# The side work of the second mixers: other slots for softplus, the norm and the sums of the two directions

## What is computed

```
xz = xn @ Win;  xi, z = split(xz)                      # 512 features each
xi = silu(causal_conv4(xi) + convb)
dt_in, B, C = split(xi @ Wx)                           # 16, 16, 16
dt = softplus(dt_in @ Wdt + bdt)
h[t] = exp(dt[t] * A) * h[t-1] + dt[t] * xi[t] * B[t]  # 16 states for each feature
y[t] = sum over states of h[t] * C[t]  +  xi[t] * D
out = (y * silu(z)) @ Wout
yf = layernorm(mixer_fw(xn) + xn);  yb = layernorm(flip(mixer_bw(flip(xn))) + xn)
y = yf + yb                                            # then the feed-forward part
```

## Time and profile before

| | before |
|---|---|
| median of 3 runs | 3462.02 us |
| the profiled execution | 3458.87 us |
| its span, first to last instruction | 3457.1 us |
| mean granted TensorE clock | 0.920 of full speed |
| busy, share of the span: PE, DVE, POOL, ACT | 81%, 82%, 65%, 51% |
| the passes 0 to 7 of `mixer1` | 1000.8 to 2984.2 us |
| the mixers' tail, to the next stage's first instruction | 2984.2 to 3027.5 us |

### The profile page before, as it was taken

One profiled execution on the slowest core, in us unless ns is written; L12 is line 12 of the kernel. 1 busy time (PEld: TensorE's weight loads), 2 busy tenths in 40 slices (PEclk: granted clock), 3 DMA queues, 4 the chain that ended last, 5 costly groups with the idle time before them and its releaser, 6 DMA issues. The chain is left out here.

```text
span 3457.1 us, 25114 instructions
## 1 busy us (share of the span) xinstructions
PE 2799.2 (81%) x7782; PEld 1191.0 (34%) x7782; DVE 2831.2 (82%) x2257; ACT 1773.3 (51%) x2375; POOL 2241.1 (65%) x1102
## 2 busy tenths in 40 slices
PE   6678777666578988988888888788898897778899
PEld 2223222454223333333333333333333332234344
DVE  6999999542369999999999999999999999678300
ACT  5775776231355655655655555555555654333211
POOL 3696499001339898898888888888888989401000
PEclk8899899887789999999999999999999999989899
DMA  1011011147425454554554545544545546321000
GB/s 65 31 49 37 26 49 49 60 165 274 161 87 176 177 175 162 176 184 157 186 188 160 188 169 180 171 173 168 181 167 170 190 153 207 122 89 49 12 19 24
DMA packets 164437, 451.46 MB, mean 131 GB/s; under 512 B 22832, under 2 KB 51696, under 8 KB 164272
## 3 DMA queue, kind: packets, MB, share of 16 engines
q1 hardware_dynamic: 158544, 428.89, 36.3%
q0 software_dynamic: 5760, 20.97, 1.5%
HBM read 414.94 MB, written 34.87 MB: 130 GB/s over the span
## 5 line engine op out<-in xcount | busy, mean ns | idle before, releaser
L1398 POOL TENSOR_TENSOR mix_prod<-mix_spread,mix_h 128x1024 f32<-128x1024 f32 x512 | 1344.1, 2628 | 242.9 <-DVE mix_h L1824 161.1
L1932 PE MATMUL mix_banks<-mix_prod,kept_ident 128*128 128x512 f32 x2048 | 1041.0, 634 | 67.0 <-POOL mix_prod L1398 37.3
L1448 ACT ACTIVATE mix_side_in<-mix_dt,mix_neg_a 128x1024 f32<-128x1024 f32 x384 | 437.5, 1141 | 307.9 <-DVE mix_h L1824 304.0
L1932 PEld LDWEIGHTS mix_banks<-mix_prod,kept_ident 128*128 128x128 f32 x2048 | 401.1, 200 | 499.0 <-issue 303.6
L1810 DVE TENSOR_TENSOR mix_banks<-mix_banks,mix_dtu 128x1024 f32<-128x1024 f32 x384 | 467.2, 1217 | 8.0 <-POOL mix_dtu L1388 4.1
L1824 DVE TENSOR_TENSOR_SCAN mix_h<-mix_side_in,mix_state,mix_banks 128x1024 f32<-128x1024 f32 x192 | 450.6, 2347 | 17.8 <-issue 0.5
L1824 DVE TENSOR_TENSOR_SCAN mix_h<-mix_side_in,mix_banks 128x1024 f32<-128x1024 f32 x192 | 439.1, 2287 | 18.8 <-ACT mix_side_in L1448 1.3
L410 POOL TENSOR_TENSOR mix_drive<-mix_drive,mix_du 128x1024 f32<-128x1024 f32 x128 | 305.0, 2400 | 147.9 <-ACT mix_drive L481 147.9
L1922 PE MATMUL mix_banks<-mix_parts,kept_sel 96*128 96x512 bf16 x384 | 156.1, 407 | 233.3 <-DVE mix_h L1824 226.4
L1408 POOL TENSOR_TENSOR mix_side_in<-mix_spread,mix_dtu 128x512 f32<-128x512 f32 x256 | 339.1, 1324 | 0.2
L633 DVE TENSOR_TENSOR_SCAN mix_h<-mix_banks,mix_state,mix_drive 128x1024 f32<-128x1024 f32 x128 | 296.2, 2340 | 11.5 <-POOL mix_drive L410 5.9
(11 more groups left out here) (270 smaller groups left out, 4463.1 us busy)
## 6 DMA issues: line engine op xcount, KB each, us to landing
mix_spread<-par_rows SPq DMA_DIRECT2D x640, 512.0 KB, 4.0
mix_c_row<-c_rows SPq DMA_DIRECT2D x40, 512.0 KB, 3.6
exa_f<-f SPq DMA_DIRECT2D x32, 512.0 KB, 6.7
slot_outputs<-exa_inter POOLq DMA_DIRECT2D x32, 512.0 KB, 7.4
ln_zp<-slot_outputs SPq DMA_DIRECT2D x8, 2048.0 KB, 8.0
first_acc<-xT SPq DMA_DIRECT2D x8, 512.0 KB, 7.3
x_scratch<-first_acc POOLq DMA_DIRECT2D x8, 512.0 KB, 3.2
fw_scratch<-mix_res SPq DMA_DIRECT2D x8, 512.0 KB, 6.3
```

Of the source, the lines that this page charges most:

```text
L1398: pool.tensor_tensor(prod[:, un % 2, :], spread[:, i % SLOTS, :], h[:, un % HR, :], ALU.mult).then_inc(prod_ready, 1)
L1448: act.activation(drive[un % 2] if pooled(un) else side_in[:, un % 2, :], dt[:, at // NS, :], ACT.Exp, scale=neg_a[:, way(p), at:at + 1]).t ...
L1932: mm = pe.matmul(y_bank[:, hf, :], k.ident[:], half(prod[:, un % 2, :], hf), start=False, stop=True, skip_group_check=True)
```

## The change

Only the tables of slots change. No instruction is added, removed or altered, and every engine's buffers stay what they are.

- VectorE: softplus of group 2 goes from slots 19, 19, 20 to 19, 20, 21, of group 3 from 24, 25, 26 to 25, 26, 27. The norm of the first half: `near_root` 17 to 18, `root_of` 20 to 22, `normed` 21 and 22 to 23 and 24, `joined` 32 and 33 to 38 and 45. Of the second half: `near_root` 29 to 30, `root_of` stays at 40, `normed` 46 and 47 to 43 and 44, `joined` 48 and 49 to 51 and 52. The taps of the convolution (31 to 33, 35 to 37, 39, 41, 42) and the gates stay.
- ScalarE, TensorE and `Steps`: what feeds these goes one slot later: the dt rows of group 3 (20 to 21), the fourth `out` (22 to 23) and its copy (25 to 26), the second `var` (26 to 27) and `roots` (27 to 28), the first two `xi` (25, 27 to 26, 28), their copies and the first `first_tap`.
- GpSimd: the second half of `times_u` of group 3 goes from slot 46 to 42.
- SyncE: the first load of yf goes from slot 26 to 30, the first store from 36 to 46, the second load from 37 to 46, the second store from 53 to 54.

```diff
--- before.py
+++ after.py
@@ -1134,16 +1134,16 @@
         for p in range(-1, passes + 1):
             order = []
             if 0 <= p < passes:
-                for g, s in ((1, 1), (2, 10), (3, 20)):
+                for g, s in ((1, 1), (2, 10), (3, 21)):
                     order += [(s, h, ("dt", p, g, h)) for h in range(2)]
                 for g, at in enumerate(((12, 13), (29, 30), (44, 45), (55, 56))):
                     order += [(at[h], 2, ("z", p, g, h)) for h in range(2)]
             if p >= 1:
-                for n, s in enumerate((3, 6, 16, 22)):
+                for n, s in enumerate((3, 6, 16, 23)):
                     order.append((s, 0, ("out", p - 1, n % 2, n // 2)))
-                order += [(15, 0, ("var", p - 1, 0)), (26, 0, ("var", p - 1, 1))]
+                order += [(15, 0, ("var", p - 1, 0)), (27, 0, ("var", p - 1, 1))]
             if p + 1 < passes:
-                for n, s in enumerate((25, 27, 32, 33, 34, 36, 37, 39)):
+                for n, s in enumerate((26, 28, 32, 33, 34, 36, 37, 39)):
                     order.append((s, 0, ("xi", p + 1, n // 2, n % 2)))
                 order += [(41, 0, ("cv", p + 1, 0)), (42, 0, ("cv", p + 1, 1))]
                 order.append((47, 0, ("par", p + 1)))
@@ -1318,13 +1318,12 @@
 
             def side(p, s):
                 if p >= 1:
-                    if s == 26:
+                    if s == 30:
                         load_yf(p - 1, 0)
-                    if s == 36:
+                    if s == 46:
                         store(p - 1, 0)
-                    if s == 37:
                         load_yf(p - 1, 1)
-                    if s == 53:
+                    if s == 54:
                         store(p - 1, 1)
                 if p + 1 < NP and s == 55:
                     sp.wait_ge(c_kept, p + 2)
@@ -1411,7 +1410,7 @@
                     ins.then_inc(pooled_ready, 1)
 
             def side(p, s):
-                for g, at in ((1, (10, 14)), (2, (22, 26)), (3, (34, 46))):
+                for g, at in ((1, (10, 14)), (2, (22, 26)), (3, (34, 42))):
                     if 0 <= p < NP and s in at:
                         times_u(p, g, at.index(s))
                 if p + 1 < NP and s in (60, 62):
@@ -1596,7 +1595,7 @@
                 if own and s % NS == 2:
                     skip(p, s // NS)
                 if own:
-                    for g, s0 in ((1, 2), (2, 11), (3, 21)):
+                    for g, s0 in ((1, 2), (2, 11), (3, 22)):
                         if s == s0:
                             soft_in(p, g)
                         if s == s0 + 1:
@@ -1604,22 +1603,22 @@
                         if s == s0 + 2:
                             soft_log(p, g)
                 if behind:
-                    for n, s0 in enumerate((6, 9, 19, 25)):
+                    for n, s0 in enumerate((6, 9, 19, 26)):
                         if s == s0:
                             keep_out(p - 1, n % 2, n // 2)
                     if s == 16:
                         roots(p - 1, 0)
-                    if s == 27:
+                    if s == 28:
                         roots(p - 1, 1)
                 if ahead:
                     if p + 1 == WAY and s == 5:
                         tap_matrices(1)
-                    for n, s0 in enumerate((26, 28, 33, 34, 35, 37, 38, 40)):
+                    for n, s0 in enumerate((27, 29, 33, 34, 35, 37, 38, 40)):
                         if s == s0:
                             keep_xi(p + 1, n // 2, n % 2)
                     if s in (43, 44):
                         keep_cv(p + 1, s - 43)
-                    for g, s0 in enumerate((28, 34, 37)):
+                    for g, s0 in enumerate((29, 34, 37)):
                         if s == s0:
                             first_tap(p + 1, g)
                 for s0, gate, shaped in ((14, 0, ()), (31, 1, ()), (40, None, (0, 1)), (46, 2, (2, 3)), (57, 3, ())):
@@ -1760,7 +1759,7 @@
                 if behind:
                     if s == 2:
                         gate_y(p - 1, 3)
-                    for hf, at in enumerate(((17, 20, 21, 22, 32, 33), (29, 40, 46, 47, 48, 49))):
+                    for hf, at in enumerate(((18, 22, 23, 24, 38, 45), (30, 40, 43, 44, 51, 52))):
                         if s == at[0]:
                             near_root(p - 1, hf)
                         if s == at[1]:
@@ -1771,7 +1770,7 @@
                             if s == at[4 + c]:
                                 joined(p - 1, hf, c)
                 if own:
-                    for g, at in ((1, (7, 8, 9)), (2, (19, 19, 20)), (3, (24, 25, 26))):
+                    for g, at in ((1, (7, 8, 9)), (2, (19, 20, 21)), (3, (25, 26, 27))):
                         for part, s0 in enumerate(at):
                             if s == s0:
                                 soft(p, g, part)
@@ -1936,22 +1935,22 @@
             def side(p, s):
                 own, ahead, behind = 0 <= p < NP, p + 1 < NP, p >= 1
                 if own:
-                    for g, s0 in ((1, 1), (2, 10), (3, 20)):
+                    for g, s0 in ((1, 1), (2, 10), (3, 21)):
                         if s == s0:
                             step_rows(p, g)
                     for g, at in enumerate(((12, 13), (29, 30), (44, 45), (55, 56))):
                         if s in at:
                             zg(p, g, at.index(s))
                 if behind:
-                    for n, s0 in enumerate((3, 6, 16, 22)):
+                    for n, s0 in enumerate((3, 6, 16, 23)):
                         if s0 <= s < s0 + 3:
                             project(p - 1, n % 2, n // 2, s - s0)
                     if s == 15:
                         var(p - 1, 0)
-                    if s == 26:
+                    if s == 27:
                         var(p - 1, 1)
                 if ahead:
-                    for n, s0 in enumerate((25, 27, 32, 33, 34, 36, 37, 39)):
+                    for n, s0 in enumerate((26, 28, 32, 33, 34, 36, 37, 39)):
                         if s == s0:
                             xi(p + 1, n // 2, n % 2)
                     if s in (41, 42):
```

## The result

| | before | changed |
|---|---|---|
| median, us | 3462.1 (4 runs, 3459.9 to 3465.8) | **3426.0** (4 runs, 3421.1 to 3429.2) |
| ratio of the times | | **0.989** (95%: 0.988 to 0.991) |
| profiled execution, its time | 3458.9 | 3423.6 |
| its span | 3457.1 | 3421.8 |
| first drive of pass 0 to the last scan's start | 1981.1 | 1942.5 |

The kernel is 36 us faster; 39 were forecast as the sum, 3423 as the median. The span shows where: the passes lost 38.6 us, pass 0 began 1.7 later, the tail grew by 2.1, the last stage lost 0.6, together 35.4 (by the unrounded spans 35.3).

The account below looks back on a forecast made before the run. VectorE was taken to bound the kernel, some instructions stretched by sharing a slot with GpSimd's product. Gains of 13.9, 15.2, 7.8 and 10.0 less losses of 3.5, 2.5 and 2.1 gave 38.8 us: 3423 us, range 3412 to 3439.

Parts of the forecast that it names:

- L1707: Softplus's second part, moved from slot 19 to 20, falls to 1.20 us each in passes 1 to 7: gain 13.9 us.
- L1710: Softplus's third part, moved from slot 20 behind L1729 (`root_of`) to slot 21, falls to 1.20 us: gain 15.2 us.
- The norm: Second half's norm, moved from slots 46 and 47 to 43 and 44, loses its stretching by GpSimd's backlog: gain 7.8 us.
- Joins and taps: Joins leave slots 32 and 33, SyncE's load goes to slot 30, so convolution taps are no longer stretched: gain 10.0 us.
- The gate: With `near_root` moved behind the gate in slot 18, VectorE waits there for TensorE's sum: loss 3.5 us.
- Rival 3: TensorE isn't binding at the gate: 3.9 us gained there, 3.5 not lost; 3416 us, chance 0.10.
- The port in slots 19 to 27: Nine SBUF instructions in a row leave VectorE and GpSimd level, and VectorE pays where early: loss 2.5 us.
- rival 1: GpSimd falls behind and the port paces slots 19 to 27, 15.8 us lost in place of 2.5; 3436.5 us, chance 0.15.
- rival 2: TensorE's slow clock makes VectorE wait for spread rows once a pass in slots 12-18 or 28-31: 3434 us, chance 0.10.
- SyncE: Store of slot 46 waits for slot 45's join in passes 5 to 7; product 46 starts 1-2 us late: cost 0.
- Rival 5: GpSimd is behind throughout slots 19 to 27 and each of nine instructions pays 1.0 us: 3484 us, chance 0.04.
- The tail: After the passes, the second half's root and norm stand ahead of the first half's second join: loss 2.1 us.

Follow-up runs that it names:

- pair19: Changed kernel with softplus's second part for group 2 back in slot 19 behind the first part: 3437.6 us.
- root21: Changed kernel with `root_of` of the first half back in slot 21, together with softplus's third part: 3447.7 us.
- norm46: Changed kernel with the norm of the second half back in slots 46 and 47 and the half of `times_u` in slot 46: 3421.2 us.
- norm47: Changed kernel with the norm of the second half in slots 47 and 48, behind ScalarE's silu block: 3420.5 us.
- join32: Changed kernel with the joins of the first half back in slots 32 and 33, their store and load in 36 and 37: 3429.6 us.
- load26: Changed kernel with SyncE's first load of yf back in slot 26: 3444.1 us.
- near17: Changed kernel with `near_root` of the first half back in slot 17, ahead of the gate: 3420.9 us.
- near29: Changed kernel with `near_root` of the second half back in slot 29: 3428.0 us.
- best2: Changed kernel with `near_root` of the first half in 17, its second join in 43, the second half's norm in 47 and 48: 3415.0 us.

## Why the prediction was right

The time came out as forecast: 3426 against 3423, inside the range, in the direction given 0.94. Its terms, in its own order:

- **L1707: right.** 12.5 us for 13.9. The 1.4 missing are pass 0, where it took 1.59 and 2.31 us. `pair19` shows the cause.
- **L1710: right**, 15.2 us to the decimal; `root21` gives 15.2 back.
- **The norm: the step that failed.** The instruction was rightly sized (7.5 us for 7.8), but slots 43 to 53 took 0.2 us more where 5.7 less were forecast. The step costed the product and its port and didn't ask what is late next when VectorE comes 2.7 us sooner: the decay behind ScalarE's silu block, for which the scan of slot 48 waits 7.0 us in passes 1 to 6. This could be read beforehand. The block's two table loads stood in the trace of before, and in pass 3 the decay behind it had 1.66 us to spare where 2.7 were taken away. `norm46` and `norm47` show both sides. Pass 7 prepares no next pass and has no such wait; there L1735 met products of GpSimd in flight, took 1.05 and 1.80 us in slots 43 and 44, and the stretch grew by 1.7 us.
- **Joins and taps: right**, 10.5 us for 10.0. That a join ahead of a tap is the cause holds (`join32`, slot 33), but only where the product is on time (slot 32). In slot 45 the join took 0.83 and 1.35 us in passes 5 and 6, and without it 43 to 53 of passes 5 to 7 are 3.4 us shorter (`join32`), where 2.1 were counted. The blame put on SyncE for the taps in slot 31 is borne out by `load26`, where they take 1.71 and 1.76 us again; what the same wait costs once softplus ends a slot later was underrated by far, at 2 to 8 us for 22.
- **The gate: right.** TensorE is binding: the waits are 6.5 us over seven passes, slots 16 to 19 grew by 2.7 where 3.5 were forecast, and `near17` takes 3.1 off. Rival 3 falls.
- **The port in slots 19 to 27: oversized.** 2.5 us forecast. In passes 1 to 7 the instructions of slots 19 to 21, 26 and 27 are all at 1.20 us. The loss there is 1.7 us, in slot 25, and from another cause, TensorE's slow clock in slot 23 of three passes. So rival 1 didn't happen. Nor did rival 2 as it was put, since the waits for the spread rows fell; its cause, the slow clock, shows in another place, at 1.7 and not 10.6 us, and by way of GpSimd.
- **The bank of z: right at 0** (`near29`). **SyncE: right at 0 in the changed kernel.** Its store waited 4.4 to 5.1 us for the join in slot 45, where some 2 were forecast, but only in pass 6 did product 46 come late by it, by 1.4 us, and VectorE didn't wait for it. Rival 5, GpSimd behind throughout, shows nowhere.
- **The tail: right**, 2.1 us for 2.1. The last norm stands ahead of the first half's second join (2982.58), and the last load behind it:

```profile
2981.25 1.42 DVE L1735 SCALAR_TENSOR_TENSOR mix_res<-mix_res,mix_norm_s,mix_logv 128x512 f32<-128x512 f32 x2
2982.58 0.75 DVE L1749 SCALAR_TENSOR_TENSOR mix_res<-mix_res,mix_norm_s,mix_lin 128x512 f32<-128x512 f32 x1
...
2983.77 0.47 SPq L1317 DMA_DIRECT2D mix_lin<-fw_scratch  x1
...
2988.06 1.42 DVE L1749 SCALAR_TENSOR_TENSOR mix_res<-mix_res,mix_norm_s,mix_lin 128x512 f32<-128x512 f32 x2 [4.73 <-DMA mix_lin<-fw_scratch]
```

That is the timeline of the changed kernel behind pass 7. The last joins wait 4.73 us where they waited 2.63.

Why the total was right although a term of 7.8 failed: other things that I hadn't counted, or had counted too dear, gave most of it back. The gate and the port took 1.6 us less than forecast, VectorE's waits for the spread rows fell from 3.4 to 1.2 (2.0 of it in pass 0, which no term had), and its 1.5 us of idle time ahead of softplus went. VectorE's instructions became 42.7 us shorter in sum and its waits 7.6 longer, which is 35.0 of the 38.6 us; the rest lies in shorter gaps and overlaps between neighbours. So the steps were right but for one, and that the total hit so closely is in part luck.

**Open.** Why pass 0 begins up to 8.5 us apart from one profiled execution to another was not followed up; it adds to the scatter of the medians. `best2` gained 3.1 us more in slots 43 to 53 than `norm47`, 2.3 of it in the passes with a join, which points to the join in 43 in place of 45; that was not tried alone. In the norm's move, GpSimd's `times_u` went along from slot 46 to 42, and no run moves that alone.

## What to carry to other kernels

Where VectorE and GpSimd share a slot, an instruction with two SBUF operands is free only as the first behind the event that releases both, and only while GpSimd has no work left from the slot before: look for a mean that is a product of GpSimd too long, and spread such instructions one to a slot. Each microsecond taken from the bounding engine is worth what the next-latest engine has to spare at that place, so before counting it, read the slack of every input of the next instructions, long blocks such as table loads above all. When a producer moves a slot later, look at every queue in which something waits for it: what stands behind it there may cost more than the move gains.

## What the runs showed of the hardware

- The lead that decides is 0.16 us: an instruction of VectorE that starts 0.16 us ahead of GpSimd's product takes 1.20 us and makes the product 3.25; one that starts 0.42 to 0.47 us behind it takes 3.01 to 3.38.
- An instruction with one operand in PSUM (`near_root`, 0.66 us) doesn't slow GpSimd's product (2.35 us), yet it costs the one behind it 1.8 us.
- A load that held SyncE's queue up to 14.9 us, three times, cost 22 us, for the lateness went through GpSimd, TensorE and VectorE in turn. In the kernel before it held the queue up to 10.1 us, and slots 28 to 34 had at most some 2 us to lose by it (17.0 less the 8.4 of the four taps, the 4.2 of the joins that moved away, and 2.2 of pass 0).
- In slot 23 of pass 3 TensorE's granted clock was 0.50 behind a wait of 2.7 us, and a sum took 3.05 us in place of 1.88; the loss came to VectorE two slots later, through GpSimd.
